# Bias rows added by GpSimd and VectorE instead of TensorE, and routing steps, square roots and a mask moved

## The reference

```python
xn = layernorm(x)                                  # x: 16 x 256 x 128, 4096 rows
q, k, v = heads(xn @ Wq + bq), heads(xn @ Wk + bk), heads(xn @ Wv + bv)   # 16 heads of 8
qp, kp = relu(q @ rw) + 1e-6, relu(k @ rw) + 1e-6  # 64 features a head
kv = kp^T v ;  norm = qp . sum(kp)
attn = (qp kv / (norm + 1e-6)) @ Wo + bo
logits = xn @ wr + br ;  top1 = argmax ;  gate = p1 / (p1 + p2)
ffn = gate * (gelu(xn @ w1[e] + b1[e]) @ w2[e] + b2[e])    # e = top1, 128 -> 512 -> 128
out = x + attn + ffn
```

## Time and profile before

| | |
|---|---|
| median of 3 executions | 260.04 us (259.35 to 261.4) |
| profiled execution | 258.03 us, span 256.3 us |
| busy TensorE | 211.7 us, 83% of the span |
| busy VectorE, ScalarE, GpSimd | 121.3, 125.4, 114.6 us |
| moved by DMA | 34.12 MB |

### The profile page before, as it was taken

How to read it: one execution, slowest core, us unless ns; L and a number is a source line. 1 busy time by engine, 2 the same in 40 slices (tenths; PEclk the granted TensorE clock), 3 DMA queues, 4 the chain that set the end, 5 groups by cost and what they waited for, 6 DMA issues and landing times.

```text
span 256.3 us, 6785 instructions
## 1 busy us (share of the span) xinstructions
PE 211.7 (83%) x2370; PEld 170.2 (66%) x2370; DVE 121.3 (47%) x386; ACT 125.4 (49%) x291; POOL 114.6 (45%) x170
## 2 busy tenths in 40 slices
PE   0499897566899999999999689288799999999920
PEld 0365664344577676667776578187799999999920
DVE  4737532577777776777676424113233333333210
ACT  2184496333565555566655544124355555555500
POOL 3984460113667444444443425205545544445540
PEclk9999999799999999999999979769999999999995
DMA  5539999700341111111111321275888878887100
GB/s 127 157 120 345 335 278 284 207 3 12 86 146 55 64 44 42 44 44 44 43 44 64 79 72 34 63 212 145 224 259 222 234 206 236 244 237 193 57 18 0
DMA packets 27749, 34.12 MB, mean 133 GB/s; under 512 B 5523, under 2 KB 19127, under 8 KB 27718
## 3 DMA queue, kind: packets, MB, share of 16 engines
q1 hardware_dynamic: 24372, 27.24, 38.9%
q0 software_dynamic: 2944, 6.37, 7.2%
q10 hardware_dynamic: 402, 0.09, 0.2%
HBM read 22.11 MB, written 14.12 MB: 141 GB/s over the span
## 4 chain that ended last, share of the span: by engine, by line
PE 68%; DVE 8%; DMA 7%; issue 4%; ACT 4%; SPq 3%; POOL 3%; ACTq 0%; POOLq 0%; DVEq 0%
PE feat L584 12%; PE feat L480 7%; PE o_bank L598 6%; PE kv_bank L491 6%; PE kt_bank L598 6%; PE feat L469 5%; PE o_bank L515 5%; PE o_bank L524 3%; PE w_bank L533 3%; PE feat L440 2%; DVE k_feat L860 2%; DMA slot_rows<-sorted_r 2%; DMA w_slot<-w1x 2%; PE feat L441 2%; PE kt_bank L500 1%
## 5 line engine op out<-in xcount | busy, mean ns | idle before, releaser
L737 ACT ACTIVATE q_all<-feat,w_slot 128x128 f32<-128x128 f32 x156 | 44.5, 368 | 48.4 <-PE feat L584 48.4
L417 POOL DMA_INDIRECT out<-k_all,slot_rows x39 | 38.3, 983 | 47.1 <-DVE k_all L934 29.0
L584 PE MATMUL feat<-xsT,w_slot 128*128 128x128 f32 x312 | 43.4, 285 | 7.8 <-DMA w_slot<-w1x 7.8
L584 PEld LDWEIGHTS feat<-xsT,w_slot 128*128 128x128 f32 x312 | 39.6, 199 | 8.8 <-DMA w_slot<-w1x 8.3
L386 POOL DMA_INDIRECT sorted_r<-rows_all,place_i x22 | 21.9, 996 | 17.8 <-PE feat L480 13.8
L694 ACT ACTIVATE k_feat<-feat 128x1024 f32<-128x1024 f32 x16 | 16.4, 1025 | 23.5 <-PE feat L469 23.5
L701 ACT ACTIVATE q_feat<-feat 128x1024 f32<-128x1024 f32 x16 | 16.4, 1027 | 22.8 <-PE feat L480 22.8
L867 DVE TENSOR_SCALAR q_feat<-feat 128x1024 f32<-128x1024 f32 x16 | 19.6, 1225 | 14.5 <-PE feat L480 14.5
L480 PE MATMUL feat<-q_all,rw_bd 32*128 32x256 f32 x256 | 19.3, 417 | 7.6 <-DVE k_feat L860 7.6
L598 PE MATMUL o_bank<-w_sb,q_all 128*128 x160 | 22.7, 286 | 0.0
L860 DVE TENSOR_SCALAR k_feat<-feat 128x1024 f32<-128x1024 f32 x16 | 19.5, 1221 | 5.2 <-PE feat L469 5.2
(11 more groups left out here) (139 smaller groups left out, 354.1 us busy)
## 6 DMA issues: line engine op xcount, KB each, us to landing
w_slot<-w1x SPq DMA_DIRECT2D x39, 258.0 KB, 3.7
sorted_r<-ones_f SPq DMA_DIRECT2D x1, 5070.0 KB, 19.9
slot_rows<-sorted_r SPq DMA_DIRECT2D x31, 130.0 KB, 3.4
x_all<-in_x SPq DMA_DIRECT2D x8, 256.0 KB, 3.3
w1x<-in_w SPq DMA_DIRECT2D x1, 2048.0 KB, 25.7
slot_rows<-sorted_r SPq DMA_DIRECT2D x16, 65.0 KB, 2.7
out<-k_all,slot_rows POOLq DMA_INDIRECT x39, 3.2
sorted_r<-rows_all,place_i POOLq DMA_INDIRECT x22
```

The source lines that it names most:

```text
L417: pool.indirect_dma_start(out_rows, bass.IndirectOffsetOnAxis(ap=slot_rows[j % SLOT_RING][:, D + 1:XW].bitcast(I32), axis=0), y_sb[j % Y_R ...
L584: ins = pe.matmul(bank[:, a * P:(a + 1) * P], w1_slot[j % W1_RING][:, a * P:(a + 1) * P], xsT[j % X_RING][:, :], start=True, stop=True)
L737: act.activation(hidden_T[j % H_RING][:, a * P:(a + 1) * P], hid_bank[j % HID][:, a * P:(a + 1) * P], ACT.Gelu, bias=w1_slot[j % W1_RING][ ...
```

## The change

Four things. The ones matmuls with their bias rows go, with `split_rows`, the first of which GpSimd did before its first normalising. Biases are loaded as tiles in which every partition holds the same row (a DMA whose source step over partitions is 0), on ScalarE's queue. The v bias is added by GpSimd in `spread_v`, the router's by VectorE in the new `find_top`, the output bias by GpSimd into x (`add_out_bias`), the second expert bias by VectorE into the slot's residual (`bias_res`: a register read of the expert's number, then bias times gate plus residual). The square root of chunk c+3 stands behind the evictions of chunk c, and an exponential that loads its table stands in chunk 5. The head mask is made while x is loaded. The last pick and the running count go behind pass 0's k ReLU, the list of earlier rows behind its q ReLU, and counting, placing, naming and the first moves each one pass later, with five moves in pass 2 and five in pass 3 instead of three, three and four in passes 1 to 3.

```diff
-EARLY_X = {1: range(K * MERGED, K * MERGED + 3), 2: range(K * MERGED + 3, K * MERGED + 6), 3: range(K * MERGED + 6, TILES)}
+EARLY_X = {2: range(K * MERGED, K * MERGED + 5), 3: range(K * MERGED + 5, TILES)}
...
+        bias_vro = sb("bias_vro", [P, VW + D], F32)
+        bias_v, bias_r, bias_o = bias_vro[:, 0:D], bias_vro[:, D:VW], bias_vro[:, VW:VW + D]
+        b2_all = sb("b2_all", [P, E * D], F32)
...
             load_x(2)
-            sp.wait_ge(vr_parts, 1)
-            sp.wait_ge(zeroed, 3)
-            for n in range(3):
-                sp.dma_start(bias_vro[n:n + 1, :].rearrange("a (p e) -> a p e", e=E),
-                             comp_part[n][0:BP, COMP2:CW]).then_inc(vro_in, 16)
...
             pool.memset(ones_b[:, :], 1.0).then_inc(consts_ready, 1)
+            pool.iota(row_i[:, :], [[0, 1]], base=0, channel_multiplier=1).then_inc(mask_ready, 1)
...
-            pool.wait_ge(vr_in, 16 * 3)
-            split_rows(slice(COMP2, CW)).then_inc(vr_parts, 1)
             normalise(0)
...
-                pool.tensor_copy(v_ones[b % 2][:, :, :, 0:HD],
-                                 v_all[:, K * b:K * (b + 1), 0:D].rearrange("p k (c d) -> p k c d", d=HD)).then_inc(v_spread, 1)
+                pool.tensor_tensor(v_ones[b % 2][:, :, :, 0:HD],
+                                   v_all[:, K * b:K * (b + 1), 0:D].rearrange("p k (c d) -> p k c d", d=HD),
+                                   strided(bias_v, [(0, K), (HD, NC), (1, HD)]), ALU.add).then_inc(v_spread, 1)
+
+            def add_out_bias(b):
+                pool.tensor_tensor(x_all[:, b, :], x_all[:, b, :], strided(bias_o, [(0, K), (1, D)]), ALU.add).then_inc(x_biased, 1)
...
                 out_bias(b)
                 if b + 2 < NBATCH:
                     spread_v(b + 2)
-                if b == 1:
+                add_out_bias(b)
+                if b == 2:
                     pool.wait_ge(placed, 2)
...
-                        pe.matmul(v_bank[h][:, k, :], ones_b[:, :], bias_vr, start=True, stop=False)
...
-                    pe.matmul(wo_bank[:, k * D:(k + 1) * D], ones_b[:, :], bias_o, start=True, stop=False)
...
-                if i == 0:
+                if i == 1:
                     pe.wait_ge(spread, 2)
...
-                pe.matmul(bank, ones_b[:, :], b2_rows[:, bass.ds(e * D, D)], start=True, stop=False)
...
+            act.dma_start(bias_v, every_row(bv)).then_inc(vro_in, 16)
+            act.dma_start(bias_r, every_row(br)).then_inc(vro_in, 16)
+            act.dma_start(bias_o, every_row(bo)).then_inc(vro_in, 16)
...
+            act.dma_start(b2_all[:, :], every_row(b2.rearrange("e d -> (e d)"))).then_inc(b2_in, 16)
...
             for c in range(CHUNKS):
-                if c + 3 < CHUNKS:
-                    deviation(c + 3)
                 if c + 1 < CHUNKS:
                     save_xnT(c + 1)
                 save_qk(c, 0)
                 save_qk(c, 1)
+                if c == CHUNKS - 3:
+                    act.activation(warm[:, :], ln_eps[:, :], ACT.Exp)
                 for h in range(CB):
                     save_v(c, h)
+                if c + 3 < CHUNKS:
+                    deviation(c + 3)
...
+            def find_top(n):
+                dve.wait_ge(v_saved, (n + 1) * RT // K)
+                if n == 0:
+                    dve.wait_ge(vro_in, 16 * 3)
+                then(dve.tensor_tensor(logits[:, n * RT:(n + 1) * RT, :], logits[:, n * RT:(n + 1) * RT, :],
+                                       strided(bias_r, [(0, RT), (1, E)]), ALU.add))
+                for t in range(n * RT, (n + 1) * RT):
+                    ins = dve.max(top8[:, t, :], logits[:, t, :])
+                steps[0] += 1
+                ins.then_inc(route, 1)
...
+                if c % 2 == 1:
+                    find_top(c // 2)
+                    if c + 1 < CHUNKS:
+                        pick(c // 2)
...
                 k_relu(i)
+                if i == 0:
+                    pick(CHUNKS // 2 - 1)
+                    scan_rows()
                 if i >= 4:
                     residual(i - 4)
                 q_relu(i)
+                if i == 0:
+                    list_earlier()
                 if i >= 2:
                     token_rows(i - 2)
                 mask_kv(i)
-                if i == 0:
+                if i == 1:
                     count_slots()
-                if i == 1:
+                if i == 2:
                     place_rows()
-                if i == 2:
+                if i == 3:
                     name_experts()
...
+            def bias_res(j):
+                dve.reg_load(b2_reg[j % 2], expert_no[0:1, j:j + 1])
+                e = dve.snap(b2_reg[j % 2], min_val=0, max_val=E - 1)
+                if j < AHEAD:
+                    dve.wait_ge(r_in[j], 16)
+                else:
+                    dve.wait_ge(slot_in[j % SLOT_RING], 16 * (j // SLOT_RING + 1))
+                res = slot_rows[j % SLOT_RING][:, XW:XW + D]
+                dve.scalar_tensor_tensor(out=res, in0=b2_all[:, bass.ds(e * D, D)], scalar=slot_rows[j % SLOT_RING][:, D:D + 1],
+                                         in1=res, op0=ALU.mult, op1=ALU.add).then_inc(res_ready, 1)
...
                 if j == EARLY + 1:
+                    dve.wait_ge(b2_in, 16)
+                    for n in range(EARLY):
+                        bias_res(n)
                     for n in range(EARLY):
                         add_res(n)
+                if j >= EARLY + 1:
+                    bias_res(j - 1)
+            bias_res(SLOTS - 1)
```

More of the change, by code:

```diff
@@ L800, in normalise @@
                 ins.then_inc(xn_dve, 1)
-            for c in range(3):
-                row_stats(c)
-                row_scale(c)
-                normalise(c)
-            dve.memset(b2_rows[:, :].bitcast(F32), 0.0).then_inc(zeroed, 1)
-            for c in range(CHUNKS):
-                if c + 3 < CHUNKS:
-                    row_stats(c + 3)
-                    row_scale(c + 3)
-                    normalise(c + 3)
-                if c % 2 == 1:
-                    pick(c // 2)
-            flat = lambda m: m[:, :, :].rearrange("p e t -> p (e t)")
-            dve.wait_ge(mask_ready, 3)
-            then(dve.tensor_tensor_scan(flat(upto), flat(keep), flat(onehot), 0.0, ALU.mult, ALU.add))
-            dve.tensor_tensor(earlier[:, :, :], upto[:, :, :], onehot[:, :, :], ALU.subtract).then_inc(spread, 2)
-            dve.tensor_tensor(gate_d[:, :], top8[:, :, 1], top8[:, :, 0], ALU.subtract).then_inc(gate_in, 1)
             dve.wait_ge(mask_ready, 1)
```

83 lines of the change are left out of this document (35 added, 48 removed).

## The result

The changed kernel takes 251.69 us (median of 4, 251.2 to 252.79), the kernel before 259.94 beside it (4 runs, 259.35 to 261.4): ratio 0.9691, 95% interval 0.9639 to 0.9744. The forecast of 249.5 was 2.2 us too low. The two profiled executions are only 5.2 us apart (258.03 and 252.79, spans 256.3 and 251.1): that of before lies 1.9 under its median, that of after is the slowest of its four and 1.1 above its median.

What follows compares the result with a forecast made beforehand. Bounds: waits between engines in the projections, VectorE at attention's start, TensorE in passes 4 to 15 and from slot 9. Terms summed to 10.5 us off the 260.04 median, giving 249.5 us, range 244.5 to 257.5.

Steps and rivals of the forecast that it cites:

- Projections, +3.9: Projection chunks: earlier first normalising, fewer bias matmuls and the head mask made during the x wait save 3.9 us.
- Rival (c): Projections gain nothing, since ScalarE's root, now last, and the picks set a chunk at TensorE's old time; 253.5 us, chance 0.15.
- First ReLU, +3.2: Start of attention: of VectorE's 4.17 us before its first ReLU only search, 0.66, and bias, 0.3, remain; saves 3.2 us.
- pass 0, +1.1: First attention pass: matmuls at full clock rate, a pass of 5.8 us; saves 1.1 us, bound 1.4.
- Passes 1 to 3, -0.7: Early attention: these passes now also hold counting, 1.41 us, less 0.7 us of VectorE slack in pass 3; loses 0.7 us.
- rival (a): Expert stage: VectorE becomes the bound through bias_res, at 1.6 us each if additions wait out GpSimd's puts; 264 us, chance 0.1.
- Passes 4 to 15, +2.5: Later attention: two bias matmuls fewer on TensorE save 0.23 us a pass, 11 times; 2.5 us.
- rival (b): Attention: GpSimd becomes the bound if an output-bias addition takes 1.6 us; 258 us, chance 0.1.
- Into the experts, +1.0: Last four projections and first slots: eleven biases, 1.2 us, partly eaten by GpSimd's row moves; saves 1.0, bounds 0 and 1.3.
- Block and clock, -2.4 and -1.5: Slot 5: four bias_res ahead of the residual additions cost 2.4 us; the idle TensorE's lower clock costs 1.5 more.
- Slots, +3.4: Expert slots from slot 9 on: 30 bias matmuls fewer at 0.112 us each save 3.4 us.
- (d): Expert stage stays at 2.0 us a slot because the queues are the limit; 253 us, chance 0.13.

Runs made afterwards that it cites:

- dummy_bias: Changed kernel with one bf16 matmul put back at each place where a bias matmul was, the additions staying on VectorE and GpSimd; 271.07 us, ratio 1.0207.
- bias_late: Changed kernel with the v, router and output bias loads issued behind the second square root instead of at the start; ratio 0.973.
- after_again: The changed kernel, unchanged, run and profiled once more in a later set; 262.60 us, ratio 0.9847.
- roots_back: Changed kernel with chunk c+3's square root again at a chunk's start; chunk 2's turn to first k features 25.46 us, against 23.71 in the changed kernel.
- add_late: Changed kernel with GpSimd's output-bias additions kept out of passes 0 to 2 and caught up later; 1.2 us slower than after_again.
- split: Changed kernel with late bias loads, early bias_res, early row moves spread thinner from pass 3, row placing cut over passes 2 and 3, naming in pass 4; 245.87 us.
- res_early: Changed kernel with the bias additions of slots 0 to 3 done around an earlier gating, not in one block before the residual additions; ratio 0.973.
- before_again: The kernel before the change, unchanged, traced once more; q features of pass 0 at 48.40 us, passes 0 to 4 last 39.0 us.

## Why the prediction was right, and where it was off

The direction, the mechanism and the range held: TensorE's matmuls were the price that counted (dummy_bias), no rival took over, and the time is inside 244.5 to 257.5. That the forecast came within 2.2 us is in part luck: in the two traces 5.5 us came of the 10.5 in the sum, and the medians lie 8.2 apart because before was profiled 1.9 below its median and after 1.1 above. By the steps, in the profiled executions:

- **Projections, +3.9: 0.34 came.** Three things made the difference. First, the turn of chunk 1 came at 12.07 and not 10.33. 1.59 of the 1.74 us is the late x load, to which I gave 0 with a bound of 0.5; bias_late shows it, at 1.50 for this turn (10.53 for after_again's 12.03) and 1.24 for pass 0. The bound was the fault: I looked at the loads' bytes, and not at what is in flight beside the very first load. Second, TensorE ran at half rate for longer in chunk 1: from its turn to chunk 2's are 6.05 us, where I took 4.51, before's 4.96 less the biases. The products of 128x512 take 1.91 and 1.92 us there and 1.02 from 18.56 on; in after_again the second takes 1.32 (16.70 for 18.12, from turns at 12.03 and 12.07). The granted clock of the profile stands at 1.00 in the whole stretch and does not show this, so that it is a late rise of the clock is my reading of the durations. In the other twelve traces this stretch has 4.45 to 5.57, so about 1.4 us is luck of the single execution. Third, from chunk 2 on the walk was right (23.71 for 23.31, where the kernel before took 26.33). Rival (c), nothing gained here, was right on the number of this trace and wrong on its reason: from chunk 2's turn to the first k features 2.6 us were gained, and roots_back puts the moved root at 1.75 of them; they were lost again ahead of chunk 2.
- **First ReLU, +3.2: 3.35**, and **pass 0, +1.1: 1.29** (6.97 to 5.68, at full clock). Right.
- **Passes 1 to 3, -0.7: -3.6.** The second largest miss. Four parts make 3.3 of the 3.6. In pass 1 counting took 2.23 us (53.56 to 55.79) where I took 1.41. In pass 2 placing took 3.03 (60.77 to 63.80) where before had 2.57, and it starts 3.61 behind the pass's q features where before had 3.16, since `token_rows` now stands in front of it. In pass 3 the clock was low (PEclk in the stretch below): from its q features to its k features TensorE took 4.68 us (65.11 to 69.79), before 3.11. I had charged the counting, less pass 3's slack, and had taken every other step at its old price and the clock as high; a low clock where I took it high was the last of my own signs of being wrong. But TensorE was waiting for VectorE in passes 1 and 2, so whatever VectorE's steps grew by was added to the pass. That the idle time of 2.90 us brought the low clock is not shown: in after_again the same waits of 2.04 and 2.90 us stand ahead of passes 2 and 3, and there the features of pass 2 are slow (1.60) and those of pass 3 are not (1.15). In all traces of the changed kernel and its variants at least one such stretch falls into passes 1 to 3.

Busy times of the changed kernel by stretch: PE, PEld, DVE, ACT, POOL, then PEclk, DMA share, GB/s.

```profile
60.00:65.00 5.00, 2.20 (x39) 1.14 (x32) 4.75 (x14) 1.84 (x3) 2.70 (x4) 1.00 0.02 5
65.00:70.00 5.00, 4.89 (x60) 3.70 (x64) 1.97 (x4) 1.63 (x2) 2.98 (x4) 0.66 0.12 40
```

The lengthened steps lie beside GpSimd's additions, and each ends within 0.04 us of one: a scan of 128x8 took 0.59 for 0.25, an addition of 128x8 took 0.64 for 0.17, and in pass 2 a cast of 128x32 took 0.62 for 0.18, nearly all of the 0.46 that placing grew by. The Trainium skill, "SBUF — State Buffer", Who interferes with whom, has a rule by which a VectorE instruction with two SBUF inputs contends with a GpSimd instruction that reads SBUF. I had weighed it for the expert stage (rival (a)) and not here. The trace agrees with it for the scan and the addition, and add_late shows it for the addition, 0.17 once GpSimd's is gone. The cast has one input, so this rule doesn't name it, but it is held up in the same way: 0.18 in add_late and 0.17 in split, where no addition of GpSimd stands beside it, and 0.61 to 0.64 in the other nine traces of the changed kernel and its variants. It works the other way too: `spread_v` took 0.94 us in pass 2 and not 0.74, started 0.09 behind a VectorE step of two inputs (61.31 and 61.22).

- **Passes 4 to 15, +2.5: 1.43.** A pass saved 0.13 and not 0.23. The price of a bias matmul was lower here than in the slots: four f32 steps and two biases took 0.77 us (103.44 to 104.21), the four steps alone 0.64 (107.36 to 108.00), so 0.065 each. I carried the slot's 0.11 over. VectorE was not the cause: dummy_bias gives the 0.13 back a pass. On GpSimd the additions took 0.73 to 0.75 for 0.65; rival (b) needed 1.6, but add_late shows that one addition more in a pass is felt.
- **Into the experts, +1.0: 1.41.** Just above its upper bound of 1.3. The longest wait of TensorE in both kernels lies here, 6.16 us before and 6.11 now for w1 of the first slots, and the change does not touch it.
- **Block and clock, -2.4 and -1.5: -2.1 together, the biases of slots 5 to 11 included.** The additions start 2.46 later against the gate (2.73 for 0.27), as forecast, by 0.56 a bias_res. The slots' own gain and slack in the chain gave a part back: slot 9's features are at 180.15, 2.53 before the old 182.68, those of slot 12 at 186.67 against 188.80. The clock cost 1.8 (two groups at 1.99 and 1.89 for 1.06), near the 1.5 assumed. TensorE's idle time was 2.84 us and not 4. res_early puts the whole at 2.9.
- **Slots, +3.4: 3.4** from slot 12 on (2.13 ahead there, 5.56 at the last step), of which 27 x 0.11 = 3.0 are the biases. VectorE works 7.25 of 14 us there, 1.0 a slot for the 1.25 to 1.6 forecast, and bounds nothing; rivals (a) and (d) fall.
- **The exponential's table:** 1.28 us, loaded under the projections, and the next activation follows at once, with none of the drain that the prediction names; the time would not have shown it, since the load is hidden.

```profile
32.72 1.28 ACT L666 ACT_TABLE_LOAD   x1
34.02 0.20 ACT L666 ACTIVATE warm<-ln_eps 128x1 f32<-128x1 f32 x1
```

(These two rows are bias_late's.) In sum 0.3 + 3.35 + 1.3 - 3.6 + 1.4 + 1.4 - 2.1 + 3.4 = 5.5 us at the last VectorE step; 0.3 of it is lost behind it, since the last puts, 1.3 apart, follow GpSimd and not VectorE.

Left open: what stops VectorE and ScalarE for 2 to 4 us in the first two sets and not in the third, and whether fewer moves in a row would shorten it. The first and the third set have the same chip number on record, so it is not a property of the chip alone. Stops and low clock together take about as much from both kernels in attention (passes 0 to 4 longer by 7.0 and 7.2 us), and the ratio is worse by 1.6% there all the same. The table shows where that lies: from the last q features to the residual additions after_again takes 36.50 us and after 34.76, from there to the last step 68.98 and 67.70; before_again and before differ by 0.2 us or less in both. What lengthens these two stretches in the changed kernel alone was not followed.

## What to carry to other kernels

Work taken off the bound engine pays back what it took from start to start in that place, so read the price in the very stage, before the same neighbour. Work that is moved to idle engines must be laid against the stretches in which those engines, or their neighbours on the same memory, are late; the average share of busy time says nothing of that. And loads put beside a kernel's first transfer can delay everything behind it: here 132 KB on another queue cost 1.2 to 1.6 us.

## What the runs showed that I had not expected

- Three broadcast loads at the start (64, 4 and 64 KB) delayed the first 256 KB x load by 1.5 to 1.6 us, although they were issued behind it and on another queue.
- A VectorE instruction of 128x8 elements took 0.64 us and not 0.17 beside a GpSimd addition of 128x256, and a cast of 128x32 0.62 and not 0.18.
- A register read on VectorE with the instruction under it costs 0.56 us from one to the next, 0.20 of it between two.
- The moment at which TensorE gets to its full rate in the second chunk differed from trace to trace: in the changed kernel and its variants chunk 2's turn comes 4.45 to 6.05 us behind chunk 1's.
- Runs of one kernel differed by 4% between sets (251.69 and 262.60), with stops of VectorE and ScalarE in attention that end 0.9 to 1.1 us after the last of GpSimd's moves that follow each other.
